# Side scans written over their own dBu with a ring of six, and four turned states instead of three, in a bidirectional Mamba block

## The reference

```python
def step(h, t):
    dA_t, dBu_t, C_t = t
    h = dA_t * h + dBu_t
    return (h, jnp.einsum('bdn,bn->bd', h, C_t))
dA = jnp.exp(delta[..., None] * A)
dBu = (delta * u)[..., None] * Bm[:, :, None, :]
y = ys + u * Dp
y = y * silu(z)
```

## Time and profile before

| | us |
|---|---|
| median of 3 runs | 7640.59 (7639.97 to 7645.27) |
| the profiled execution | 7615.24 |
| its span | 7613.5 |
| TensorE / VectorE / ScalarE / GpSimd busy | 6890.6 / 6827.7 / 6158.4 / 6966.0 |

### The profile page before, as it was taken

How to read it: one execution, slowest core, us unless ns; L and a number is a source line. 1 busy time by engine, 2 the same in 40 slices (tenths; PEclk the granted TensorE clock), 3 DMA queues, 4 the chain that set the end, 5 groups by cost and what they waited for, 6 DMA issues and landing times. The chain is left out here.

```text
span 7613.5 us, 110015 instructions
## 1 busy us (share of the span) xinstructions
PE 6890.6 (91%) x32682; PEld 4090.0 (54%) x32682; DVE 6827.7 (90%) x9069; ACT 6158.4 (81%) x12569; POOL 6966.0 (91%) x3774
## 2 busy tenths in 40 slices
PE   6899899999999999999998999999998999999889
PEld 3455555555555555555555555555555555555455
DVE  2799999999999999999999999999999999999766
ACT  1788888888888888888888888888888888888645
POOL 0899999999999999999999999999999999999778
PEclk8999999999999999999999999999999999999999
DMA  8444445344444454444445544444445444444555
GB/s 257 145 135 130 127 143 148 107 141 139 136 129 126 144 148 106 141 137 134 129 125 148 148 107 141 138 134 130 128 144 148 107 141 136 134 133 129 148 196 171
DMA packets 605392, 1064.01 MB, mean 140 GB/s; under 512 B 113584, under 2 KB 221872, under 8 KB 596336
## 3 DMA queue, kind: packets, MB, share of 16 engines
q1 hardware_dynamic: 602704, 1055.84, 47.1%
q10 hardware_dynamic: 2080, 1.05, 0.0%
HBM read 926.61 MB, written 130.05 MB: 139 GB/s over the span
## 5 line engine op out<-in xcount | busy, mean ns | idle before, releaser
L689 POOL TENSOR_TENSOR dBu<-Bb,du 128x1024 f32<-128x1024 f32 x2048 | 4783.3, 2364 | 4.8 <-DMA Bb<-bc_scratch 4.8
L1160 DVE TENSOR_TENSOR_SCAN scans<-scans,state,dBu 128x512 f32<-128x512 f32 x2304 | 2900.6, 1279 | 538.7 <-ACT scans L803 371.3
L803 ACT ACTIVATE scans<-delta,A 128x512 f32<-128x512 f32 x4096 | 2757.2, 694 | 395.8 <-DVE hC L1176 317.9
L1025 PE MATMUL yT<-ident,hC 128*128 128x128 f32 x9216 | 1409.3, 284 | 258.1 <-DVE hC L1176 254.8
L1176 DVE TENSOR_TENSOR hC<-scans,Cb 128x512 f32<-128x512 f32 x2304 | 1553.8, 679 | 0.0
L698 POOL TENSOR_TENSOR hR<-hR,Cb 128x512 f32<-128x512 f32 x1024 | 1293.0, 1274 | 279.3 <-ACT state L814 278.0
L1025 PEld LDWEIGHTS yT<-ident,hC 128*128 128x128 f32 x9216 | 1085.3, 145 | 661.7 <-DVE hC L1176 361.2
L1160 DVE TENSOR_TENSOR_SCAN hR<-scans,state,dBu 128x512 f32<-128x512 f32 x1024 | 1292.0, 1262 | 0.0
L1018 PE MATMUL bg<-u,comb 128*128 128x512 f32 x2112 | 989.1, 594 | 0.9 <-DVE u L1133 0.9
L1160 DVE TENSOR_TENSOR_SCAN hV<-scans,state,dBu 128x512 f32<-128x512 f32 x768 | 967.5, 1260 | 15.3 <-ACT scans L803 11.3
L957 PE MATMUL bg<-hT,win_u 128*128 128x512 f32 x2112 | 966.3, 598 | 0.9 <-ACT hT L725 0.9
(11 more groups left out here) (163 smaller groups left out, 7597.2 us busy)
## 6 DMA issues: line engine op xcount, KB each, us to landing
comb<-pre_scratch SPq DMA_DIRECT2D x1040, 256.0 KB, 4.6
Bb<-bc_scratch SPq DMA_DIRECT2D x264, 512.0 KB, 8.1
Cb<-bc_scratch SPq DMA_DIRECT2D x264, 512.0 KB, 7.9
win_u<-in_win SPq DMA_DIRECT2D x264, 256.0 KB, 4.7
pre_scratch<-pre SPq DMA_DIRECT2D x264, 256.0 KB, 3.7
comb<-comb_scratch SPq DMA_DIRECT2D x66, 1024.0 KB, 8.1
win_z<-in_win SPq DMA_DIRECT2D x257, 256.0 KB, 2.7
part_scratch<-pre SPq DMA_DIRECT2D x132, 256.0 KB, 2.0
```

What stands on the lines that cost most here:

```text
L689: pool.tensor_tensor(dBu[:, q % AHEAD], Bb[:, 2 * q:2 * q + 2, :], du[:, j % 2, :].unsqueeze(1).broadcast_to([P, 2, T]), ALU.mult).then_in ...
L803: act.activation(place(n)[:], delta[:, j % 2, :], ACT.Exp, scale=A[:, i % 2, j * N + n:j * N + n + 1]).then_inc(dA_made, 1)
L1025: ins = nc.tensor.matmul(yT[:, tt * P:(tt + 1) * P], product[:, tt * P:(tt + 1) * P], ident[:], start=first and tt == 0, stop=False, is_tr ...
L1160: nc.vector.tensor_tensor_scan(to, place(n)[:], dBu[:, q % AHEAD, k, :], state[:, c:c + 1], ALU.mult, ALU.add).then_inc(h_made, 1)
```

## The change

States 2, 5, 8 and 11 are turned, and 1, 4 and 7 are aside; nine states are straight as before (0, 3, 6, 9, 10, 12 to 15). All side scans are written over their own dBu in a ring of six pairs instead of four, so `hV` goes and `hR` holds GpSimd's products only. GpSimd waits for the scan itself, no longer for ScalarE's copy. Before it writes a dBu again it waits for the copy, the product or the transposes that read it. A turned state is transposed in its own pair, one earlier than before, and by the table `ORDER` it stands behind all other background work that starts at the same position. Each side state's last column is copied by itself, four states later, and the first chunk of a sequence starts its scans from 0.0, so the multiply of the states goes.

```diff
-TURNED = (1, 5, 9)
-ASIDE = (3, 4, 7, 11)
+TURNED = (2, 5, 8, 11)
+ASIDE = (1, 4, 7)
 LATE = 3
 SIDE = tuple(sorted(TURNED + ASIDE))
 STRAIGHT = [n for n in range(N) if n not in SIDE]
 NS, NA, NT = len(STRAIGHT), len(ASIDE), len(TURNED)
-COPIES = ((3, 4), (7,), (11,))
 PLACES = 4
-KEPT_WITH = {n: ns[-1] for ns in COPIES for n in ns}
-JOINS = {n: min(KEPT_WITH[n] // 2 + LATE, NQ - 1) for n in ASIDE}
-HC, HR, HV = 4, 4, 3
-AHEAD = 4
+JOINS = {n: min(n // 2 + LATE, NQ - 1) for n in ASIDE}
+HC, HR = 4, NA
+KEPT_BEHIND = 4
+AHEAD = 6
 GROUP = 32
 NG = P // GROUP
-assert MT * NS % HC == 0 and HR == NA and HV == NT
-assert all(b - a == ns[1] - ns[0] for ns in (*COPIES, TURNED) for a, b in zip(ns, ns[1:]))
-assert sorted(n for ns in COPIES for n in ns) == sorted(ASIDE)
+assert MT * NS % HC == 0 and SIDE[-1] + KEPT_BEHIND < N
@@ -79,9 +76,9 @@
 ]
 OWN_BANK = 2
 PER_TILE = [(f"Y{(j - 1) % MT}", (j * NQ,), OWN_BANK) for j in range(MT)]
-PER_TILE += [(f"T{j * N + n}", (j * NQ + n // 2 + 1,), OWN_BANK) for j in range(MT) for n in TURNED]
-FIRST = {kind: k for k, kind in enumerate("YDZT")}
-SCHEDULE = sorted(GENERAL + PER_TILE, key=lambda entry: (entry[1][0], FIRST.get(entry[0][0], len(FIRST))))
+PER_TILE += [(f"T{j * N + n}", (j * NQ + n // 2,), OWN_BANK) for j in range(MT) for n in TURNED]
+ORDER = {kind: k for k, kind in enumerate("YDZUCOXKHT")}
+SCHEDULE = sorted(GENERAL + PER_TILE, key=lambda entry: (entry[1][0], ORDER[entry[0][0]]))
 EV = len(SCHEDULE)
 AT = {name: at for name, at, bank in SCHEDULE}
...
@@ -684,18 +678,27 @@
                     for q in range(NQ):
                         p = j * NQ + q
                         pool.wait_ge(h_made, g * N + 2 * (q + 1 - AHEAD) + H0)
+                        before, pair = divmod(g * NQ + q - AHEAD, NQ)
+                        for n in (2 * pair, 2 * pair + 1):
+                            if before >= 0 and n in SIDE:
+                                pool.wait_ge(side_saved, side(before, n) + 1)
+                            if before >= 0 and n in ASIDE:
+                                pool.wait_ge(hR_made, aside(before, n) + 1)
+                            if before >= 0 and n in TURNED:
+                                pool.wait_ge(bg_ready, ready(before // MT, f"T{before % MT * N + n}"))
                         if j == 0:
                             pool.wait_ge(B_loaded[q], i * 16 + 16)
-                        pool.tensor_tensor(dBu[:, q % AHEAD], Bb[:, 2 * q:2 * q + 2, :],
+                        pool.tensor_tensor(dBu[:, ring(g, q)], Bb[:, 2 * q:2 * q + 2, :],
                                            du[:, j % 2, :].unsqueeze(1).broadcast_to([P, 2, T]),
                                            ALU.mult).then_inc(dBu_made, 1)
                         for n in ASIDE:
                             if q == JOINS[n]:
                                 k = ASIDE.index(n)
-                                pool.wait_ge(aside_saved, copied(g, n) + A0)
+                                pool.wait_ge(h_made, g * N + n + 1 + H0)
+                                pool.wait_ge(hR_used, aside(g, n) + 1)
                                 if j == 0:
                                     pool.wait_ge(C_loaded[n // 2], i * 16 + 16)
-                                pool.tensor_tensor(hR[:, k, :], hR[:, k, :], Cb[:, n, :], ALU.mult).then_inc(hR_made, 1)
+                                pool.tensor_tensor(hR[:, k, :], dBu[:, ring(g, n // 2), n % 2, :], Cb[:, n, :], ALU.mult).then_inc(hR_made, 1)
                         if q == 6:
...
@@ -803,16 +806,11 @@
                 act.activation(place(n)[:], delta[:, j % 2, :], ACT.Exp,
                                scale=A[:, i % 2, j * N + n:j * N + n + 1]).then_inc(dA_made, 1)
-            def keep_states(g, j, n):
-                for ns, places, saved in [(ns, hR, aside_saved) for ns in COPIES] + [(TURNED, hV, turned_saved)]:
-                    if n != ns[-1] + 4:
-                        continue
-                    act.wait_ge(h_made, g * N + ns[-1] + 1 + H0)
-                    k = (ASIDE if places is hR else TURNED).index(ns[0])
-                    step = ns[1] - ns[0] if len(ns) > 1 else 1
-                    act.copy(state[:, j * N + ns[0]:j * N + ns[-1] + 1:step],
-                             places[:, k:k + len(ns), T - 1]).then_inc(saved, 1)
+            def keep_state(g, j, n):
+                if n in SIDE:
+                    act.wait_ge(h_made, g * N + n + 1 + H0)
+                    act.copy(state[:, j * N + n:j * N + n + 1], dBu[:, ring(g, n // 2), n % 2, T - 1:T]).then_inc(side_saved, 1)
             nc.scalar.preload_act_table_set(EXP_LN)
             act.wait_ge(consts_made, 2)
...
@@ -874,14 +872,7 @@
                             elif p == TAKE[name] and name in MIDWAY:
                                 take_turned(ready(i, name), bank(name), TURNED[-1], s)
                         step_dA(g, i, j, 2 * q + 1)
-                        keep_states(g, j, 2 * q + 1)
-                        if q == 5:
-                            last = (j - 1) % MT
-                            act.wait_ge(state_saved, kept(g, 0) + S0)
-                            act.wait_ge(aside_saved, g * len(COPIES) + A0)
-                            act.wait_ge(turned_saved, g + V0)
-                            act.mul(state[:, last * N:(last + 1) * N], state[:, last * N:(last + 1) * N],
-                                    cur[:, C_KEEP_PREV:C_KEEP_PREV + 1]).then_inc(state_kept, 1)
+                        keep_state(g, j, 2 * q + 1 - KEPT_BEHIND)
                         if p == 12:
                             act.wait_ge(cur_loaded, i * 16 + 32)
                         for name in BY_ACT:
@@ -996,10 +987,10 @@
                                            start=True, stop=True, is_transpose=True, skip_group_check=True)
                 ins.then_inc(bg_ready, 1)
-            def transpose_state(bank, g, j, n):
+            def transpose_state(bank, g, n):
                 pe.wait_ge(h_made, g * N + n + 1 + H0)
                 for tt in range(TT):
-                    ins = nc.tensor.matmul(bank[:, tt * P:(tt + 1) * P], hV[:, TURNED.index(n), tt * P:(tt + 1) * P],
+                    ins = nc.tensor.matmul(bank[:, tt * P:(tt + 1) * P], dBu[:, ring(g, n // 2), n % 2, tt * P:(tt + 1) * P],
                                            ident[:], start=True, stop=True, is_transpose=True, skip_group_check=True)
                 ins.then_inc(bg_ready, 1)
@@ -1056,7 +1047,7 @@
                             turn_back(bank, i * MT + p // NQ - 1, k, s if k < MT - 1 else 1 - s, sk + 16 * (k % 2),
                                       freed(i if k < MT - 1 else i - 1, f"T{k * N + TURNED[-1]}"))
                         if kind == "T":
-                            transpose_state(bank, i * MT + p // NQ, k // N, k % N)
+                            transpose_state(bank, i * MT + k // N, k % N)
                         if kind == "U":
                             project_u(bank, i + 1, k, 1 - s, part(KD))
...
@@ -1138,7 +1129,8 @@
                 s = i % 2
                 for j in range(MT):
                     g = i * MT + j
-                    dve.wait_ge(state_kept, g - 6 + K0)
+                    if i % CH_SEQ:
+                        dve.wait_ge(side_saved, side(g - MT + 1, 0))
                     for q in range(NQ):
                         p = j * NQ + q
                         dve.wait_ge(state_saved, kept(g, q) + S0)
@@ -1147,18 +1139,9 @@
                             n = 2 * q + k
                             c = j * N + n
                             dve.wait_ge(dA_made, g * N + n + 1 + DU0)
-                            if n in ASIDE:
-                                dve.wait_ge(hR_used, aside(g, n) + 1)
-                                to = hR[:, ASIDE.index(n), :]
-                            elif n in TURNED:
-                                dve.wait_ge(bg_ready, ready(i if j else i - 1, f"T{((j - 1) % MT) * N + n}"))
-                                dve.wait_ge(turned_saved, g + V0)
-                                to = hV[:, TURNED.index(n), :]
-                            else:
-                                to = place(n)[:]
-                            nc.vector.tensor_tensor_scan(to, place(n)[:], dBu[:, q % AHEAD, k, :],
-                                                         state[:, c:c + 1], ALU.mult, ALU.add).then_inc(h_made, 1)
+                            to = dBu[:, ring(g, q), k, :] if n in SIDE else place(n)[:]
+                            nc.vector.tensor_tensor_scan(to, place(n)[:], dBu[:, ring(g, q), k, :],
+                                                         state[:, c:c + 1] if i % CH_SEQ else 0.0, ALU.mult, ALU.add).then_inc(h_made, 1)
                         if q == 1:
                             name = f"Y{(j - 1) % MT}"
                             gate(ready(i, name), bg[OWN_BANK], g - 1, (j - 1) % MT, s if j else 1 - s)
```

(19 more changed lines are left out.)

## The result

The changed kernel takes 7936.04 us (median of 4 runs, 7931.26 to 7938.19), the kernel before 7640.28 beside it: 1.0386 times, 95% interval 1.0368 to 1.0404, so 296 us slower. The forecast was 7990. The profiled execution has a span of 7936.0 us, 322.5 more than before.

What follows compares the result with a forecast made beforehand. Shares named no bound; VectorE is held by GpSimd (0.63 us a tile) and ScalarE (1.0), the latter at the tile's end. Terms 2.8 + 6.3 + 0.8 + 1.0 = 10.9 us a chunk, 32 chunks, 349 us: 7990, range 7700 to 8120.

Steps and rivals of the forecast that it cites:

- The end of the tile is what counts: Tile's end, where ScalarE stops for two table loads: VectorE's wait there for ScalarE matters more than its 1.0 us a tile.
- Tile 5, +6.3: C5 behind U7 delays C6's row load 3.8 us, state 11 stands behind C6: table load 6.3 us later a chunk.
- Tile 2, +2.8: State 11 stands behind U1 on TensorE and ScalarE takes it before dA 15: table load 2.8 us later.
- Tile 6, +0.8: State 5's take moves ahead of the mid-tile table loads: 1.00 more, less 0.32 idle, 0.1 for copies: +0.8 us.
- The other five, +1.0: Remaining five tiles: GpSimd stall removed, -0.63, against an unabsorbed take plus part of TensorE's, +1.3; +0.2 each, +1.0 us.
- GpSimd's relief is worth 0 to 0.63 us a tile: VectorE's stall for GpSimd's last dBu should go; alone worth 0 to 0.63 us a tile, as ScalarE's wait may remain.
- The fourth turned state nets to 0 on ScalarE: One more take on ScalarE, 1.00 us, and copies about 0.1, against dA 6 sliding into idle time: net 0 a tile.
- What sorting does: The order on TensorE counts in two places: state 11 behind U1 in tile 2, C5 behind U7 in tile 5.
- GpSimd was the bound: Rival, faster: GpSimd's 0.63 us a tile disappears, ScalarE's idle time swallows the take; 161 us less, 7480; chance 0.14.
- Only tiles 2 and 6: Rival: tile 5 costs only 0 to 2.6 us; 7790 to 7870, or 7700 with the others at -0.4; chance 0.19.
- The low clock spreads: Rival: tile 5's longer wait keeps TensorE at low clock to tile's end, 3 us more a chunk, 8085; chance 0.10.

Runs made afterwards that it cites:

- The kernel with the old states: The changed kernel with the states (turned 1, 5, 9; aside 3, 4, 7, 11), transpose positions and sorting of before: 7538.72 us, in a second group 7540.62.
- the sorting mended: The changed kernel with the old sorting, but H ahead of the turned states: 7675.90 us; with state 11 then made an aside state: 7573.22 us.
- two runs: The changed kernel with turned states early again: with the old sorting throughout, 7757.75 us; with U still ahead of C, 7870.10 us.
- the kernel with the turned states one pair late: The changed kernel with H ahead in the sorting, three turned states (2, 5, 8; 11 aside), transposed one pair later than their own: 7847.48 us.

## Why the prediction was right, step by step

- *The end of the tile is what counts.* Right: all of the loss is in waits for dA at scan 15, at the next scan 0 or behind tile 6's table loads, and VectorE's busy time stayed.
- *Tile 5, +6.3.* Measured +6.30. Step by step: C5 stands behind U7 (shown by the row), the load is issued 0.5 us after C5's matmuls end and not held by U6's store, C6 starts 6.65 us after the issue (6.77 before), C6 itself takes 1.86 where I had 1.13, state 11 takes 0.91 at the low clock, ScalarE's table load comes 5.46 us after C6's start; I had 4.4. The wait for C6's rows is 5.24 us; over 5 was forecast. That the sum agrees so closely is luck. Counted from the gate before it (medians, 1000 to 5000 us), U6's last matmul starts 0.9 us earlier than before, where I had no change; the rows' load goes out 3.1 later and C6 starts 3.4 later, where I had 3.8 for both; and the path from C6 to the table load is longer than I had by what C6 came earlier, so that the table load is 6.3 later. VectorE idles 5.7 + 3.2 = 8.8 us at the end of the tile, more than the 7 forecast.
- *Tile 2, +2.8.* Measured +2.61, with scan 15 waiting 1.3. U1's last matmul starts 0.44 us later after the gate, half of the 0.88 that I had; part of the rest came back behind it.
- *Tile 6, +0.8.* Measured +0.49: the term was 0.3 too large.
- *The other five, +1.0.* Measured -0.16. This is the step that was mis-sized, 1.2 us a chunk or 37 us, most of the 54 us between forecast and median. Tile 0 alone gained 1.27: it lost not only GpSimd's stall of 0.6, which I had allowed it, but also the 0.7 at the next scan 0. In tiles 1 and 7 a wait for dA of 1.7 and 1.2 us came in place of the stall of 1.1. The forecast had also read a wait for ScalarE behind GpSimd's in tile 1, where there was none over 0.3, and a wait for GpSimd in tile 3, where there was none.
- *GpSimd's relief is worth 0 to 0.63 us a tile.* The kernel with the old states gives 99 / 256 = 0.39 a tile, for this and all else that is left of the change. That lies inside the bound but doesn't measure the relief alone, and the forecast said little of how much of it would be real.
- *The fourth turned state nets to 0 on ScalarE.* Not borne out: with the sorting mended it costs 103 us against an aside state. In the changed kernel it may have been inside the terms of the tiles, since ScalarE waited there anyway; no run shows that.
- *What sorting does.* The reasoning looked only for places where the new order is worse. It missed that with four turned states it is better in tile 7, by 2.7 us; the expectations of two runs missed that too.
- *Rivals.* "GpSimd was the bound" is out: its stall went and the time rose. "Only tiles 2 and 6" is out: tile 5 is two thirds of the loss. "The low clock spreads" is out: two groups behind C6 the adds are at 0.60 us again (1759.45).

## What to carry to other kernels

Where an engine works through a written order and does background work for others, the place of a small, urgent item behind a large one that somebody waits for late costs the whole large one; look at who takes the item and what stands behind that take, here one dA and two table loads. Before moving a step, list for each shared buffer which of its two conditions (the store, the last reader) is the later one and by how much: here a margin of 1.4 us turned into a delay. And when a change bundles three ideas, run each alone: here the scans over their own dBu, with the ring of six and what belongs to them, were worth 99 us (with a ring of four, all of it together cost 139), and the sorting that came with them cost more than twice that.

## What the runs showed of the hardware

A scan that starts from the constant 0.0 is shorter than one that starts from a column in SBUF. VectorE's groups in the kernel with the old states (busy us, mean ns):

```profile
L1143 DVE TENSOR_TENSOR_SCAN dBu<-scans,state,dBu 128x512 f32<-128x512 f32 x1568 | 1957.2, 1260 | 12.6 <-ACT scans L806 9.7
...
L1143 DVE TENSOR_TENSOR_SCAN dBu<-scans,dBu 128x512 f32<-128x512 f32 x224 | 266.0, 1199 | 3.7 <-ACT scans L806 3.5
```

It is 61 ns of 1260. That it is the constant, and not the chunk, is shown by the run with the column of zeros, where the same 224 scans take 1261:

```profile
L1145 DVE TENSOR_TENSOR_SCAN dBu<-scans,zero,dBu 128x512 f32<-128x512 f32 x224 | 279.8, 1261 | 1.6 <-ACT scans L808 1.3
```

A scan over its own input in SBUF takes no longer here than one into another tile (1260 and 1262 ns); in the changed kernel its mean is 1268.

TensorE's clock fell behind a wait of only 1.98 us for a bank, not only behind the waits of 3 us and more for DMA. The window of the kernel with the turned states one pair late, behind that wait (columns as in the window above; the granted clock is the 0.63):

```profile
1840.50:1845.00 4.50, 4.50 (x17) 2.62 (x15) 4.47 (x8) 3.84 (x11) 4.42 (x4) 0.63 0.00 0
```

A mean of 0.63 is a stretch at 1.2 GHz and then one at 2.4; from 1830 to 1838 us and from 1850 to 1858 us the clock is 1.00. The Trainium skill ("TensorE: Matmul & The Clock Gate", section "HAM oscillation — how this bites in real kernels") tells of this for waits on DMA; here it fell behind a wait for another engine too.
